# The last batch of an attention layer, divided by its row sums after the product with the values

## The reference, cut to what matters

```python
qkv = hidden_states @ qkv_w + qkv_b            # hidden_states: layer norm of x
q, k, v = heads of qkv;  q, k = _rope(q), _rope(k)
scores = einsum("bhqd,bhkd->bhqk", q, k) * scale + (1 - causal) * MASK_VAL
probs  = softmax(scores, axis=-1)
ctx    = einsum("bhqk,bhkd->bqhd", probs, v)
x = x + ctx @ out_w + out_b
```

## Time and profile before

| what | us |
|---|---|
| median of 3 runs (lowest, highest) | 1877.82 (1872.31, 1882.22) |
| the profiled execution's own time | 1872.54 |
| its span | 1870.7 |
| TensorE busy | 1760.0 (94%) |
| VectorE busy | 1115.4 (60%) |
| ScalarE busy | 1087.4 (58%) |
| GpSimd busy | 912.1 (49%) |
| mean granted clock | 0.984 |

### The profile page before, as it was taken

One profiled execution on the slowest core, in us unless ns is written; L12 is line 12 of the kernel. 1 busy time (PEld: TensorE's weight loads), 2 busy tenths in 40 slices (PEclk: granted clock), 3 DMA queues, 4 the chain that ended last, 5 costly groups with the idle time before them and its releaser, 6 DMA issues.

```text
span 1870.7 us, 32100 instructions
## 1 busy us (share of the span) xinstructions
PE 1760.0 (94%) x11076; PEld 1527.0 (82%) x11076; DVE 1115.4 (60%) x3334; ACT 1087.4 (58%) x3071; POOL 912.1 (49%) x1153
## 2 busy tenths in 40 slices
PE   7979999999999999999999999999989788898788
PEld 6769989989998998998999899899878566666566
DVE  5655565556456556555644655654566777777656
ACT  3346565566556656556655765655632446777843
POOL 4545544555444555455554555545522336668720
PEclk9999999999999999999999999999989998999999
DMA  4300021012002001101200210110110310000001
GB/s 136 108 16 18 6 69 35 1 46 63 1 18 74 18 6 62 41 1 40 65 6 18 61 31 1 58 51 1 35 57 23 96 46 1 2 1 24 18 7 45
DMA packets 35424, 65.78 MB, mean 35 GB/s; under 512 B 4032, under 2 KB 4672, under 8 KB 35264
## 3 DMA queue, kind: packets, MB, share of 16 engines
q1 hardware_dynamic: 35264, 63.73, 10.8%
HBM read 61.62 MB, written 2.10 MB: 34 GB/s over the span
## 4 chain that ended last, share of the span: by engine, by line
PE 71%; DVE 9%; ACT 8%; issue 7%; POOL 5%; DMA 0%; SPq 0%; POOLq 0%; DVEq 0%; ACTq 0%
PE bank L357 55%; PE bank L974 5%; PE bank L961 4%; PE bank L976 3%; ACT s L1079 2%; POOL s L1795 2%; PE bank L1510 1%; PE bank L1481 1%; PE bank L1497 1%; DVE h L676 1%; ACT s L1566 1%; ACT W L256 1%; POOL WF L269 1%; POOL W L269 1%; POOL rstd L322 1%
## 5 line engine op out<-in xcount | busy, mean ns | idle before, releaser
L357 PE MATMUL bank<-W,oT 128*128 128x512 f32 x1632 | 432.7, 401 | 1.0 <-DVE oT L1747 1.0
L1286 POOL TENSOR_TENSOR qk<-work,qk 128x512 fp32r<-128x512 f32 (+1 forms) x160 | 193.5, 1209 | 445.9 <-ACT qk L1070 445.9
L357 PEld LDWEIGHTS bank<-W,oT 128*128 128x128 f32 x1632 | 290.1, 190 | 49.3 <-issue 1.3
L1086 ACT COPY pt<-bank 128x384 f32<-128x384 f32 x256 | 122.1, 477 | 329.8 <-PE bank L961 329.5
L1079 ACT ACTIVATE s<-s,neg_max 128x128 f32<-128x128 f32 (+1 forms) x512 | 227.6, 445 | 54.3 <-DVE neg_max L1193 52.1
L1278 POOL TENSOR_TENSOR work<-work,table 128x512 f32<-128x512 f32 (+1 forms) x160 | 191.3, 1196 | 139.1 <-ACT work L1065 139.1
L357 PE MATMUL bank<-W,xnA 128*128 128x320 f32 (+1 forms) x1056 | 186.3, 333 | 3.2 <-DVE xnA L342 2.9
L1170 DVE TENSOR_TENSOR work<-bank,table 128x512 f32<-128x512 f32 (+1 forms) x160 | 102.0, 637 | 132.3 <-ACT work L1065 132.3
L357 PEld LDWEIGHTS bank<-W,xnA 128*128 128x128 f32 x1056 | 166.8, 188 | 16.6 <-DVE xnA L342 4.1
L357 PE MATMUL bank<-xnA,W 128*128 128x256 f32 (+1 forms) x1080 | 162.1, 300 | 8.2 <-DVE W L262 6.8
L357 PE MATMUL bank<-xnB,W 128*128 128x256 f32 (+1 forms) x1080 | 164.3, 302 | 3.3 <-DVE xnB L342 3.3
(11 more groups left out here) (106 smaller groups left out, 3507.3 us busy)
## 6 DMA issues: line engine op xcount, KB each, us to landing
raw<-in_weights SPq DMA_DIRECT2D x215, 256.0 KB, 2.7
x<-in_x SPq DMA_DIRECT2D x8, 256.0 KB, 4.8
out<-x SPq DMA_DIRECT2D x8, 256.0 KB, 2.0
row<-in_bias_rows SPq DMA_DIRECT2D x5, 256.0 KB, 2.7
table<-in_constants SPq DMA_DIRECT2D x4, 240.0 KB, 3.2
b_qk<-in_bias_rows SPq DMA_DIRECT2D x1, 512.0 KB, 3.6
b_val<-in_bias_rows SPq DMA_DIRECT2D x1, 256.0 KB, 3.0
table<-in_constants SPq DMA_DIRECT2D x1, 66.0 KB, 2.3
```

The source lines that it names most:

```text
L357: last = nc.tensor.matmul(out_ap, lhs(i), rhs(j), start=start and k == 0, stop=stop and k == 2)
L1086: nc.scalar.copy(pt0[:, k, :], bank[PT][:, 0:3 * P]).then_inc(a_pt, 1)
L1286: nc.gpsimd.tensor_tensor(lo, work[:, 2 + s, st.columns(what)], hi.bitcast(F32), ALU.subtract).then_inc(a_rope_lo, 1)
```

## The change

From step 24 on (`DIVIDED = 24`, `divided(n)`), the exponentials are not multiplied by reciprocals before they are turned. The exponential instruction no longer gives a row sum, VectorE's `inverses` and GpSimd's `normalise` are left out, and `turn` waits for the exponentials (`b_exp`). `weigh` does eight more products with the same `pt1`, whose stationary operand is a constant of ones and zeros (`ones`: 16 columns of ones for each half of a pair of heads), so that columns 256 to 511 of `OUT1` hold each head's row sum in every one of its 16 output rows. Once per group VectorE takes the reciprocal of these 128x256 numbers into `o1` and multiplies the 128x256 outputs by it (`b_inverse`, `b_divided`). ScalarE's high part is then copied from `o1` and not from the bank, and the low part is a subtraction on GpSimd and not on VectorE. The key transposes wait for `b_divided` in place of `b_o_lo`. Four small memsets on GpSimd fill `ones` before step 0.

```diff
+            ones = sb(a, "ones", [P, 2, 2 * D1])
+            o1 = sb(a, "o1", [P, 2, SEQ])
...
+        DIVIDED = 24
...
+        def divided(n):
+            return n >= DIVIDED
+
+        def sum_read(eng, group):
+            if group < 0:
+                return
+            if divided(2 * group):
+                eng.wait_ge(b_divided, group - DIVIDED // 2 + 1)
+            else:
+                eng.wait_ge(b_o_lo, group + 1)
...
-            at_least(pe, b_o_lo, group - 1)
+            sum_read(pe, group - 2)
...
-                    at_least(pe, b_o_lo, group)
+                    sum_read(pe, group - 1)
...
+                if divided(m):
+                    pe.wait_ge(b_ones, 4)
+                    for tt in range(2):
+                        for j in range(4):
+                            last = nc.tensor.matmul(bank[OUT1][rows(j), SEQ + tt * P:2 * SEQ], ones[:, odd, :],
+                                                    pt1[:, j, tt * 2 * P:(tt + 2) * P],
+                                                    start=False, stop=odd == 1 and tt == 1)
...
-                pe.wait_ge(b_norm, 4 * m + j + 1)
+                pe.wait_ge(b_exp if divided(m) else b_norm, 4 * m + j + 1)
...
+                    if divided(n):
+                        last = nc.scalar.activation(s1[:, s, cols], s1[:, s, cols], ACT.Exp, bias=bias, scale=-1.0)
+                    else:
...
+                if divided(n - 1):
+                    act.wait_ge(b_divided, group - DIVIDED // 2 + 1)
+                    nc.scalar.copy(oT1[HI][:, group % ORING, :], o1[:, group % 2, :]).then_inc(b_o_hi, 1)
+                else:
...
-            if here:
+            if here and not divided(n):
                 inverses(0)
...
+            if before and n % 2 == 0 and divided(n - 1):
+                group = n // 2 - 1
+                dve.wait_ge(b_pv, group + 1)
+                at_least(dve, b_o_lo, group - 1)
+                nc.vector.reciprocal(o1[:, group % 2, :], bank[OUT1][:, SEQ:2 * SEQ]).then_inc(b_inverse, 1)
+                dve.wait_ge(b_inverse, group - DIVIDED // 2 + 1)
+                nc.vector.tensor_tensor(o1[:, group % 2, :], bank[OUT1][:, 0:SEQ], o1[:, group % 2, :],
+                                        ALU.mult).then_inc(b_divided, 1)
...
-            if n < QUADS:
+            if n < QUADS and not divided(n):
                 normalise(0)
                 normalise(1)
...
+            if n >= 1 and n % 2 == 0 and divided(n - 1):
+                group = n // 2 - 1
+                pool.wait_ge(b_o_hi, group + 1)
+                nc.gpsimd.tensor_tensor(oT1[LO][:, group % ORING, :], o1[:, group % 2, :],
+                                        oT1[HI][:, group % ORING, :].bitcast(F32),
+                                        ALU.subtract).then_inc(b_o_lo, 1)
```

More of the change, by code:

```diff
@@ L1344, in program @@
         b_row = sem("b_row")
+        b_ones = sem("b_ones")
+        b_inverse = sem("b_inverse")
+        b_divided = sem("b_divided")
         b_added = sem("b_added")
@@ L1499, in weigh @@
                                                 pt1[:, j, tt * 2 * P:(tt + 2) * P],
-                                                start=odd == 0 and tt == 0, stop=odd == 1 and tt == 1)
+                                                start=odd == 0 and tt == 0,
+                                                stop=odd == 1 and tt == 1 and not divided(m))
+                if divided(m):
[5 more added lines that the diff above has]
+                                                    start=False, stop=odd == 1 and tt == 1)
                 if odd:
@@ L1565, in exponentials @@
                 for qt, cols in ((0, slice(0, P)), (1, slice(P, 3 * P))):
-                    last = nc.scalar.activation(s1[:, s, cols], s1[:, s, cols], ACT.Exp,
-                                                bias=b_neg_max[:, s, qt:qt + 1], scale=-1.0,
-                                                accum_out=b_row_sum[:, s, qt:qt + 1])
+                    bias = b_neg_max[:, s, qt:qt + 1]
+                    if divided(n):
+                        last = nc.scalar.activation(s1[:, s, cols], s1[:, s, cols], ACT.Exp, bias=bias, scale=-1.0)
+                    else:
+                        last = nc.scalar.activation(s1[:, s, cols], s1[:, s, cols], ACT.Exp, bias=bias, scale=-1.0,
+                                                    accum_out=b_row_sum[:, s, qt:qt + 1])
                 last.then_inc(b_exp, 1)
@@ L1585, in b_scalar_step @@
                 group = n // 2 - 1
-                act.wait_ge(b_pv, group + 1)
-                nc.scalar.copy(oT1[HI][:, group % ORING, :], bank[OUT1][:, 0:SEQ]).then_inc(b_o_hi, 1)
+                if divided(n - 1):
+                    act.wait_ge(b_divided, group - DIVIDED // 2 + 1)
+                    nc.scalar.copy(oT1[HI][:, group % ORING, :], o1[:, group % 2, :]).then_inc(b_o_hi, 1)
+                else:
+                    act.wait_ge(b_pv, group + 1)
+                    nc.scalar.copy(oT1[HI][:, group % ORING, :], bank[OUT1][:, 0:SEQ]).then_inc(b_o_hi, 1)
             if here:
@@ L1741, in b_vector_step @@
                 b_vector_biased(dve, *fill[1:])
-            if here:
+            if here and not divided(n):
                 inverses(1)
-            if before and n % 2 == 0:
+            if before and n % 2 == 0 and divided(n - 1):
[6 more added lines that the diff above has]
+                                        ALU.mult).then_inc(b_divided, 1)
+            elif before and n % 2 == 0:
                 group = n // 2 - 1
@@ L1767, in b_gpsimd @@
             pool.wait_ge(b_zero, 2)
+            for odd in range(2):
+                for half in range(2):
+                    nc.gpsimd.memset(ones[:, odd, half * D1:(half + 1) * D1],
+                                     1.0 if half == odd else 0.0).then_inc(b_ones, 1)
             for n in range(STEPS1):
```

## The result

| | before | after |
|---|---|---|
| median of 7 runs (lowest, highest), us | 1877.82 (1872.31, 1882.22) | 1888.08 (1884.81, 1893.82) |
| ratio to before, 95% interval | | 1.0063 (1.0040 to 1.0087) |
| profiled execution | 1872.54 | 1885.21 |
| its span | 1870.7 | 1883.4 |
| weigh(24) to the output product of the last batch | 48.4 | 58.8 |

The ratio is estimated from the executions of both kernels and isn't exactly the quotient of the two medians (1.0055); one slow execution each of e9 and e10 (2236 and 2997 us) is left out of theirs.

What follows compares the result with a forecast made beforehand. TensorE holds 71% of the chain, GpSimd 5%; the pace-setting loop ordinarily bypasses GpSimd. Ones +0.9 and +5.5, even steps +3.3, end +2.3, removal -1.3 and -1.05 sum to +9.7: 1877.8 becomes 1887.5, range 1880 to 1893.

Steps and rivals of the forecast that it cites:

- The loop that sets the pace: Ordinary steps bypass GpSimd; anything between weigh and scores delays copies and the next step; GpSimd releases last in steps 29, 32.
- The ones: Eight more products per step on TensorE ahead of the scores: 0.79 each for steps 26 to 32, +5.5, plus step 25.
- The first set: Ones of step 25, where the granted clock is 0.50: +0.9, taken between 0.79 and 1.43.
- The reciprocal: VectorE's 128x256 reciprocal takes 1.54, from the line through the reciprocals of 2 and 8 elements.
- the plain pass: Lower bound for the 128x256 reciprocal, 0.42; as the cheap-reciprocal rival, +5.3 in all, chance 0.24.
- The even steps: Steps 26, 28, 30: ScalarE's high part waits for the division, its copies behind it; 1.1 lost each, +3.3.
- The end: From weigh(31) to the output product 5.0 against 1.89; with the ones counted already, +2.3.
- What the removal saves: Small reciprocals and GpSimd multiplications dropped: -1.3 in step 29, -1.05 in step 32.
- the step 31: Exponentials without accumulator reading: taken as 0 because VectorE is about as late; bound -0.4.
- the sum: All terms, 0.9 + 5.5 + 3.3 + 2.3 - 1.3 - 1.05, giving +9.7.
- The clock: Rival: longer TensorE idle before weigh(26) and the output product brings the lower clock, up to 1.8 each; chance 0.19.
- the clock's case: Total if TensorE's clock falls more often: +11.5 to +13.3, 1890; chance 0.19.

Runs made afterwards that it cites:

- e9: Kernel before the change, with only GpSimd's bias addition in steps 2 and 4 of each batch moved behind its last two multiplications; ratio 1.0017.
- e10: e9 with the last step's reciprocals of heads (31, 2) and (31, 3) taken one head at a time; ratio to before 1.0022.
- e1: Changed kernel without the eight products with ones per step; 1881.57 us, ratio to before 1.0032.
- e2: Changed kernel with the 128x256 reciprocal replaced by a plain copy; 1883.08 us, ratio to before 1.0035.
- e3: Changed kernel without the products with ones and with a plain copy for the reciprocal; 1875.55 us, ratio to before 1.0000.
- e8: Changed kernel with VectorE reciprocals of several widths and a plain copy appended after the attention; 6.25 ns per element from 64 elements on.
- e5: Changed kernel with ScalarE's high part of a divided group moved behind its copies of heads (n, 0) and (n, 1); ratio to before 1.0076.
- e4: Kernel before with only the removal of row sums, small reciprocals and GpSimd multiplications from step 24 on; 1871.45 us, ratio 0.9979.
- e12: Changed kernel with idle TensorE products: 14 before the output product, 8 in steps 25 and 27, 5 in 26 and 28; ratio to before 1.0024.
- e11: e10 with idle TensorE products, 8 in steps 25 and 27 and 5 in steps 26 and 28; 1870.96 us, ratio to before 0.9983.

## Why the prediction was right, by its own steps

*The loop that sets the pace.* Right: e1 and e2 show that what is put between weigh and the scores, and what delays the copies, comes out again in the next weigh. One reading was incomplete: GpSimd is the last to release something in a third place too, before the turns of step 27 (0.60 at 1753.92 before the change). It costs nothing there, since weigh(26) then waits 1.97 for ScalarE; with the removal this stretch is no shorter (7.36 in e3, 7.40 before).

*The ones.* Right in place, a little too dear: 0.79 taken, 0.64 to 0.65 measured. The distance from weigh to the scores holds a part that two sets in a row pay once. The first set, in the low stretch, was taken at 0.9; weigh(24) to weigh(25) grew by 0.5 (8.13 to 8.61).

*The reciprocal.* Right in kind: 1.54 taken, 1.76 measured, the plain pass excluded. Two shapes of 2 and 8 elements, 32 ns apart, were enough to choose between 0.42 and 1.54; that their slope of 5.4 ns came near the 6.25 of long rows is partly luck, since e8 has 4.4 between 8 and 32 elements. e8's 6.25 ns against the plain 1.04 is six passes. The Trainium skill's repeat count of 8 ("VectorE: DVE Perf Modes", section "First, the fixed hardware budget"), read as eight passes, would have given an estimated 2.3; the measurement decides.

*The even steps.* The size held (1.1 taken, 1.23 measured), the mechanism only in part. The prediction said that the key transposes and VectorE's extremes "are ready before ScalarE's branch needs them"; e5 shows that they are nearly as late as the copies, and moving the copies gave 0.46 in one such step and nothing in another.

*The end.* 5.0 taken, 5.16 measured: the reciprocal and GpSimd's low part (0.73 for 0.64) were longer, the ones shorter. The 0.06 per signal stands in no row; the chain shows 0.02.

*What the removal saves.* -1.3 and -1.05 taken; e4 shows -1.30 and -1.14. Another 0.3 came in the step that ends with weigh(30), the step 31 for which the sum took 0 and gave -0.4 as a bound.

*The clock.* This is what the forecast left out and gave a chance of 0.19: of the two idle stretches that the rival named, the one before the output product (3.66) was followed by the lower clock (8.41), the one before weigh(26) (3.22) was not (0.86). Two that it did not name were: the clock fell in step 26, behind weigh(25) and its wait of 2.79 (the scores took 1.66), and before weigh(30) (1.51). In all it took 5.7 of the last batch, 4.1 more than before. The own cost was 8.9 where the sum had 9.7 (the ones 1.2 too dear, the removal 0.4 too small; the even steps 0.5 and the end 0.3 too cheap), so the distance plus the product grew by 13.0 and not by 9.7. On the medians the growth was 10.3, and the forecast of 1887.5 stands beside 1888.08. The interval of the ratio allows 7.5 to 16.3, so that this closeness is in good part luck: the clock's case, with 11.5 to 13.3, is the one that the trace shows.

## What to carry to other kernels

A normalisation moved behind a product has to be paid for by whatever then makes the sums: here eight more products stood on TensorE's loop, while the multiplications that they replaced lay on an engine that set the pace in two places of nine steps. Before dividing "once for eight heads", count elements and not instructions: the small reciprocals took 0.2 each for 8 columns, the new one 1.76 for 256. And a wait added before TensorE can cost twice: the 3.66 before the output product cost once as the wait and once more as products at half the clock (8.4 in place of 5.7), while the 3.22 before weigh(26) cost only itself.

## What the runs showed of the hardware that I had not expected

A set of these products (four column groups of 32) takes 0.64 to the start of another set of the same shape directly behind it, and 0.79 to the start of the scores. VectorE's fp32 reciprocal takes 6.25 ns per element from 64 elements on, from PSUM or SBUF alike. Idle stretches of nearly equal length on TensorE were followed by the lower clock in some executions and not in others (3.30 before weigh(24) in the changed kernel and 0.50 behind it, 3.22 before weigh(26) and 1.00); 8, 5, 8 and 5 idle products in four steps, with the 14 at the end, kept it at 1.00 throughout in the one execution of e12 that was traced; in e11 the same 26 did not keep it from falling once.
